# Row sums as two columns, inverted small and spread back over the partitions; attention logits moved ahead of X W2

## The reference, cut to what matters

```python
x = x + gnn(layernorm(x), adj, ...)
x = x + ffn(layernorm(x), ...)          # Mamba: scan over 1024 channels x 16 states

def gnn(X, A, Wv, bv, aw, ab, Wk, bk):  # per batch, N = 128, d = 256
    Xw = X @ Wv + bv
    sj, si = Xw @ aw[:d, 0], Xw @ aw[d:, 0]
    e = leaky_relu(sj[:, None, :] + si[:, :, None] + ab[0], 0.2)
    alpha = A * exp(e)
    transition = alpha / (sum(alpha, axis=-1, keepdims=True) + 1e-12)
    H, Xk = 0, X
    for k in range(3):
        H = H + Xk @ Wk[k] + bk[k]
        Xk = transition @ Xk
    return relu(H)
```

## Time and profile before

| | |
|---|---|
| median of 3 runs | 3949.91 us (3949.03 to 3950.27) |
| profiled execution | 3946.52 us |
| its span, first to last instruction | 3944.4 us |
| granted TensorE clock, mean | 0.979 |
| VectorE busy | 3646.4 us |
| TensorE busy | 3506.4 us |
| GpSimd busy | 3451.7 us |
| ScalarE busy | 2830.4 us |

### The profile page before, as it was taken

How to read it: one execution, slowest core, us unless ns; L and a number is a source line. 1 busy time by engine, 2 the same in 40 slices (tenths; PEclk the granted TensorE clock), 3 DMA queues, 4 the chain that set the end, 5 groups by cost and what they waited for, 6 DMA issues and landing times. The chain is left out here.

```text
span 3944.4 us, 43314 instructions
## 1 busy us (share of the span) xinstructions
PE 3506.4 (89%) x10938; PEld 1931.7 (49%) x10938; DVE 3646.4 (92%) x3133; ACT 2830.4 (72%) x6002; POOL 3451.7 (88%) x1860
## 2 busy tenths in 40 slices
PE   6789899999899999899989899989899899899887
PEld 3545455545455444455444455444455444445443
DVE  0499999999999999999999999999999999999998
ACT  1477777777777877777877777877777777677775
POOL 0298889998889998889998889998889998889999
PEclk9899999999999999999999999999999999999999
DMA  2111101111101111101111101111100111100110
GB/s 106 50 53 56 55 9 50 53 55 55 55 8 50 52 55 55 55 14 45 53 55 55 55 16 42 52 55 55 55 21 37 53 55 55 55 26 28 49 49 8
DMA packets 50715, 183.77 MB, mean 47 GB/s; under 512 B 7340, under 2 KB 33204, under 8 KB 42068
## 3 DMA queue, kind: packets, MB, share of 16 engines
q1 hardware_dynamic: 48880, 174.17, 11.5%
q10 hardware_dynamic: 1636, 7.83, 0.5%
HBM read 164.15 MB, written 17.83 MB: 46 GB/s over the span
## 5 line engine op out<-in xcount | busy, mean ns | idle before, releaser
L407 POOL TENSOR_TENSOR st<-st,bc 128x1024 f32<-128x1024 f32 x1024 | 2399.2, 2360 | 310.6 <-DVE st L843 310.5
L843 DVE TENSOR_TENSOR_SCAN st<-dec,st 128x1024 f32<-128x1024 f32 x1024 | 2310.0, 2277 | 26.6 <-ACT dec L460 20.3
L668 PE MATMUL y_ps<-st,ident 128*128 128x512 f32 x4096 | 1984.9, 613 | 309.7 <-POOL st L407 308.3
L460 ACT ACTIVATE dec<-delta,decay 128x254 f32<-128x254 f32 x4096 | 1696.8, 467 | 623.6 <-DVE st L843 608.3
L668 PEld LDWEIGHTS y_ps<-st,ident 128*128 128x128 f32 x4096 | 745.1, 192 | 1178.9 <-issue 582.2
L831 DVE TENSOR_TENSOR st<-du,bc 128x1024 f32<-128x1024 f32 x736 | 884.6, 1202 | 4.0 <-ACT du L446 4.0
L398 POOL TENSOR_TENSOR st<-du_sb,bc 128x1024 f32<-128x1024 f32 x288 | 679.5, 2360 | 0.1
L869 DVE SCALAR_TENSOR_TENSOR u<-d_ps,chan,u 128x250 f32<-128x250 f32 (+2 forms) x768 | 308.7, 472 | 68.1 <-ACT u L500 68.0
L706 PE MATMUL d_ps<-xnT,wxz 128*128 128x256 f32 x1024 | 250.5, 388 | 55.5 <-DVE u L869 55.5
L706 PEld LDWEIGHTS d_ps<-xnT,wxz 128*128 128x128 f32 x1024 | 191.0, 191 | 157.0 <-DVE u L869 107.1
L718 PE MATMUL d_ps<-xnT,wxz 128*128 128x256 f32 x1024 | 247.3, 385 | 13.6 <-ACT zs L509 13.5
(11 more groups left out here) (98 smaller groups left out, 2452.4 us busy)
## 6 DMA issues: line engine op xcount, KB each, us to landing
bc<-bc_dram SPq DMA_DIRECT2D x64, 2048.0 KB, 9.5
xg<-x_dram SPq DMA_DIRECT2D x32, 256.0 KB, 11.4
x_dram<-xg SPq DMA_DIRECT2D x32, 256.0 KB, 2.0
last_x<-x_dram SPq DMA_DIRECT2D x32, 256.0 KB, 2.6
out_dram<-last_x SPq DMA_DIRECT2D x32, 256.0 KB, 2.2
bc<-w_inT_dram ACTq DMA_DIRECT2D x1, 4096.0 KB
adjt<-adjT_dram SPq DMA_DIRECT2D x32, 128.0 KB, 11.1
bc<-w_out_dram ACTq DMA_DIRECT2D x1, 2048.0 KB
```

The costliest lines, as they stand in the source:

```text
L407: nc.gpsimd.tensor_tensor(st[:, sl, :, :, :], st[:, sl, :, :, :], bc[:, p, 1, SU * q:SU * q + SU, None, :].to_broadcast([P, SU, 2, T]), AL ...
L460: a = nc.scalar.activation(dec[:, v % 2, s, j, :].rearrange("p (b t) -> p b t", b=PAIR)[:, :, 1:], delta[:, p, 2 * i + j, :].rearrange("p ...
L668: mm = nc.tensor.matmul(y_all, ident[:, :], st[:, sl, s, :, :].rearrange("p j t -> p (j t)"), start=False, stop=(q == Q - 1 and s == SU - ...
L843: nc.vector.tensor_tensor_scan(h, dec[:, v % 2, :, :, :].rearrange("p s j t -> p (s j t)"), h, 0.0, ALU.mult, ALU.add).then_inc(S["scanned ...
```

## The change

The logits, exponentials and the product with the adjacency come first (phases 9, 11, 12). The row sums become two products with `att` of one batch as the stationary operand and one column of ones, so that they stand as two columns, one row per partition (phase 14). VectorE adds epsilon and inverts 128 x 2 elements (phase 15). X W2 follows (phase 16). ScalarE makes for each batch a diagonal matrix of the reciprocals in `xn` by scaling the identity (phase 17), then copies `x2k` (phase 18). TensorE multiplies ones with the diagonals, which spreads the reciprocals over all partitions (phase 19), and VectorE multiplies them into `att` (phase 20). The later phases move by one: 22 and 23, 25, 26 and 27, 29. ScalarE's second normalisation also waits for the spreading product, since the diagonals stand in `xn`.

```diff
         x1k = sb("x1k", [P, PAIR, DIM])
         x2k = sb("x2k", [P, PAIR, DIM])
         ones = sb("ones", [P, P])
+        rowsum = sb("rowsum", [P, PAIR])
+        rinv = sb("rinv", [P, PAIR])
         last_x = sb("last_x", [P, PAIR, DIM])
         bstat = sb("bstat", [P, PAIR, 6])
         mv = sb("mv", [P, PAIR, 2])
...
                     second = v == 33
                     wait(act, "rstd_made", 2 * g + 1 + second)
                     wait(act, "transposed", 2 * g + second)
+                    if second:
+                        wait(act, "rinv_mm", g + 1)
                     for b in range(PAIR):
                         a = nc.scalar.activation(xn[:, b, :], xg[:, p, b, :], ACT.Identity, bias=shift[:, b:b + 1],
                                                  scale=rstd[:, b:b + 1])
...
                     wait(act, "transposed", 2 * g + 1)
                     nc.scalar.activation(xT[:, :, :].rearrange("p c t -> p (c t)"), g0[:, :], ACT.Copy)\
                         .then_inc(S["xT_made"], 1)
-                if v == 11:
+                if v == 18:
                     wait(act, "x2k_mm", g + 1)
                     nc.scalar.activation(x2k[:, :, :].rearrange("p b d -> p (b d)"), g0[:, :], ACT.Copy)\
                         .then_inc(S["x2k_made"], 1)
-                if v == 14:
+                if v == 17:
+                    wait(act, "rinv_made", g + 1)
+                    for b in range(PAIR):
+                        a = nc.scalar.activation(xn[:, b, 0:P], ident[:, :], ACT.Copy, scale=rinv[:, b:b + 1])
+                    a.then_inc(S["rinv_diag"], 1)
+                if v == 11:
                     wait(act, "e_mm", g + 1)
                     nc.scalar.activation(att[:, :, :].rearrange("p b i -> p (b i)"), g0[:, 0:T], ACT.Exp, bias=c0[:, 0:1])
                     nc.scalar.activation(g0[:, T:2 * T], g0[:, 0:T], ACT.Exp, bias=c0[:, 1:2], scale=0.2)\
                         .then_inc(S["e_exp"], 1)
-                if v == 24:
+                if v == 25:
                     wait(act, "x1k_mm", g + 1)
                     nc.scalar.activation(x1k[:, :, :].rearrange("p b d -> p (b d)"), g0[:, :], ACT.Copy)\
                         .then_inc(S["x1k_made"], 1)
...
                             mm = nc.tensor.transpose(g0[:, c * T + b * L:c * T + (b + 1) * L],
                                                      xn[:, b, c * P:(c + 1) * P], ident[:, :])
                     mm.then_inc(S["transposed"], 1)
-                if v == 9:
-                    wait(pe, "xT_made", g + 1)
+                if v == 16:
+                    wait(pe, "rinv_made", g + 1)
                     for b in range(PAIR):
                         mm = hop(b, 2, True, True)
                     mm.then_inc(S["x2k_mm"], 1)
-                if v == 12:
-                    wait(pe, "x2k_made", g + 1)
+                if v == 9:
+                    wait(pe, "xT_made", g + 1)
                     for b in range(PAIR):
                         for c in range(KC):
                             cols = xT[:, c, b * L:(b + 1) * L]
...
                             mm = nc.tensor.matmul(g0[:, b * L:(b + 1) * L], cols, wj_rep[:, c, :],
                                                   start=False, stop=(c == KC - 1))
                     mm.then_inc(S["e_mm"], 1)
-                if v == 17:
+                if v == 14:
                     wait(pe, "alpha_made", g + 1)
-                    nc.tensor.matmul(g0[:, 0:T], ones[:, :], att[:, :, :].rearrange("p b i -> p (b i)"),
-                                     start=True, stop=True).then_inc(S["rowsum_mm"], 1)
-                if v in (21, 22):
-                    b = v - 21
+                    for b in range(PAIR):
+                        mm = nc.tensor.matmul(g0[:, b:b + 1], att[:, b, :], ones[:, 0:1], start=True, stop=True)
+                    mm.then_inc(S["rowsum_mm"], 1)
+                if v == 19:
+                    wait(pe, "x2k_made", g + 1)
+                    wait(pe, "rinv_diag", g + 1)
+                    for b in range(PAIR):
+                        mm = nc.tensor.matmul(g0[:, b * L:(b + 1) * L], ones[:, :], xn[:, b, 0:P], start=True, stop=True)
+                    mm.then_inc(S["rinv_mm"], 1)
+                if v in (22, 23):
+                    b = v - 22
                     wait(pe, "att_made", g + 1)
                     hop(b, 1, True, False)
                     mm = nc.tensor.matmul(g0[:, b * DIM:(b + 1) * DIM], att[:, b, :], x2k[:, b, :],
                                           start=False, stop=True, skip_group_check=True)
                     if b == 1:
                         mm.then_inc(S["x1k_mm"], 1)
-                if v in (25, 26):
-                    b = v - 25
+                if v in (26, 27):
+                    b = v - 26
                     wait(pe, "x1k_made", g + 1)
                     if b == 0:
                         nc.tensor.matmul(g0[:, :], ones3, bk_row, start=True, stop=False, skip_group_check=True)
...
                     for b in range(PAIR):
                         a = nc.vector.bn_aggr(mv[:, b, :], bstat[:, b, :])
                     a.then_inc(S["aggr"], 1)
-                if (v, late) == (15, 1):
+                if (v, late) == (12, 1):
                     wait(dve, "e_exp", g + 1)
                     nc.vector.tensor_tensor(g0[:, 0:T], g0[:, T:2 * T], att[:, :, :].rearrange("p b i -> p (b i)"),
...
                     nc.vector.tensor_tensor(att[:, :, :].rearrange("p b i -> p (b i)"), g0[:, 0:T],
                                             adjt[:, p, :, :].rearrange("p b i -> p (b i)"), ALU.mult)\
                         .then_inc(S["alpha_made"], 1)
-                if (v, late) == (19, 1):
+                if (v, late) == (15, 1):
                     wait(dve, "rowsum_mm", g + 1)
-                    nc.vector.tensor_scalar(g0[:, 0:T], g0[:, 0:T], EPS_ROW, None, ALU.add)\
+                    nc.vector.tensor_scalar(rowsum[:, :], g0[:, 0:PAIR], EPS_ROW, None, ALU.add)\
                         .then_inc(S["rowsum_eps"], 1)
                     wait(dve, "rowsum_eps", g + 1)
-                    nc.vector.reciprocal(g0[:, T:2 * T], g0[:, 0:T]).then_inc(S["rinv_made"], 1)
-                    wait(dve, "rinv_made", g + 1)
-                    nc.vector.tensor_tensor(att[:, :, :].rearrange("p b i -> p (b i)"), g0[:, T:2 * T],
+                    nc.vector.reciprocal(rinv[:, :], rowsum[:, :]).then_inc(S["rinv_made"], 1)
+                if (v, late) == (20, 1):
+                    wait(dve, "rinv_mm", g + 1)
+                    nc.vector.tensor_tensor(att[:, :, :].rearrange("p b i -> p (b i)"), g0[:, 0:T],
                                             att[:, :, :].rearrange("p b i -> p (b i)"), ALU.mult)\
                         .then_inc(S["att_made"], 1)
-                if (v, late) == (28, 0):
+                if (v, late) == (29, 0):
                     wait(dve, "h_mm", g + 1)
                     x1 = xg[:, p, :, :].rearrange("p b d -> p (b d)")
                     nc.vector.scalar_tensor_tensor(x1, g0[:, :], 0.0, x1, ALU.max, ALU.add).then_inc(S["x1_made"], 1)
```

More of the change, by code:

```diff
@@ L175, in build @@
         dec_zeroed diag_made x_loaded adj_loaded stats aggr veps_made rstd_pow rstd_made normed transposed xT_made xnT_made
-        x2k_mm x2k_made e_mm e_exp alpha_max alpha_made rowsum_mm rowsum_eps rinv_made att_made x1k_mm x1k_made
+        x2k_mm x2k_made e_mm e_exp alpha_max alpha_made rowsum_mm rowsum_eps rinv_made rinv_diag rinv_mm att_made x1k_mm x1k_made
         h_mm x1_made x1_stored x1_reloaded
```

## The result

The kernel after takes 3984.92 us (median of 4 runs, 3983.60 to 3985.47) against 3949.47 us before: ratio 1.009, interval 1.0073 to 1.0108. It is slower by 35 us; the forecast was 3943.6 us. Its profiled span is 3982.6 us, 38.2 us more than before.

The account below looks back on a forecast made before the run. The bound was taken as a loop: GpSimd's 80.4 us, 4.9 us over TensorE and ScalarE, VectorE for the rest. Steps 3 to 7 (-6.0) and the fill (-0.3) turn 3949.9 into 3943.6 us; range 3933 to 3959.

Parts of the forecast that it names:

- The new waits: Column sums at TensorE's step 24, spreading product at 29: VectorE waits 1 to 1.6 us at step 30, costing nothing.
- the hinge: Body's end: GpSimd's product of unit 30, TensorE's sum and u, ScalarE's bias, VectorE's taps of step 1; forecast not later.
- the residual: L942 on VectorE moves behind scan 6 and fills idling before the taps of step 7: -0.45 us a body.
- the fill: Bodies -3 to -1, where the graph chain is late: +1.5, -1.0 and -0.8, sum -0.3 us, bounds -3 and +3.
- GpSimd's 80.4 us: GpSimd's unbroken stretch from the product of unit 8 to that of unit 30, part of the loop setting a body's 118 us.
- VectorE's saving: 1868 ns a group, 59.8 us in all, at steps 25 to 30, before existing idling at step 1: worth zero.
- Rival (a): VectorE is the bound and its saving arrives: 3884 us, or in part 3890 to 3935; chance 0.11, whole or in part.
- The steps 3 to 7: Critical stretch: the copy +0.25, the residual -0.45, sum -0.20 us a body, -6.0 us over 30 bodies.
- the copy: ScalarE's `x1k` copy moves from step 2 to step 3, behind the gate activation: taps of step 5 come 0.25 us later.
- Rival (b): The copy at step 3 delays the taps 0.30 us a body, L942's move gives nothing: +9.0 us, 3959 us; chance 0.12.
- Rival (c): New handovers stall VectorE until GpSimd starves: 3974 us at 1 us beyond a wait of some 3 us; chance 0.07.
- The first term's sum: Body -3 in the fill: decay exponential ends at 78.83; copy 0.6, product 0.7, multiplication 0.4 give 80.6; net +1.5 us.

Follow-up runs that it names:

- e3_before_late: Kernel before with only the last phases one step later (22 and 23, 25, 26 and 27, 29), row sums and logits untouched: 3984.21 us.
- e1_late_back: Kernel after with its last phases back at their old places (21 and 22, 24, 25 and 26, residual at 28): 3953.47 us.
- e4_x1_at_29: As e1_late_back, but the residual stays at phase 29, between scans 6 and 7: 3932.34 us.
- e2_filler: Kernel after plus an unread product of X with W1 for one batch, about 1 us on TensorE, at step 31: 3941.90 us.
- e5: e4_x1_at_29 with the gate product moved from ahead of scan 2 to ahead of scan 3, and X W0 with the second hop at 26 and 27: 3935.07 us.
- e10: e4_x1_at_29 with the gate product alone moved from ahead of scan 2 to ahead of scan 3: 3970.98 us.
- e7: e4_x1_at_29 plus two unread VectorE reciprocals at phase 19, about 3.5 us a group: 3943.51 us.
- e9_before_x1_29: Kernel before with one edit, the residual at phase 29 instead of 28: 3933.94 us.
- e6_pad_1: e4_x1_at_29 plus one unread VectorE reciprocal of 128 x 256 at phase 19: 3932.18 us.

## Why the prediction was wrong

**The step that failed** is in "The new waits": "TensorE's step 31 becomes free and its work goes behind u of step 0, so the hinge is not later." I counted free time on TensorE as harmless. It was, as a queue; it was not as a clock. The pause ahead of the sum grew from 1.35 to 2.62 us, the sum and u behind it took 1.70 us more (the sum alone from 1.98 to up to 3.68), and these two are the place in the body where TensorE is on the critical path. The missing term is +1.70 us x 28 = +47.6 us. e3_before_late shows that moving the last phases makes the loss without the inversion, e1_late_back that moving them back removes it, e4_x1_at_29 that the residual has no part in it, and e2_filler that the work's use does not matter, only that it is there.

**The clock** was in the prediction, for the fill, where it was allowed 1.9 us. I did not carry it to the earlier trace rows, where a pause stood in front of a critical product. The trace of the kernel before had the warning: behind a pause of 2.64 us in the middle of the body the sum is slow in 17 of the bodies 1 to 28 (last section).

**What bounds the kernel** was right. GpSimd's 80.4 us, the hinge and VectorE's steps 1 to 8 add up to a body in every kernel here. In some bodies of e5 and e10 a late sum of TensorE reaches into GpSimd's stretch, and in ten bodies of e7 VectorE's own work is late at the hinge.

**VectorE's saving is worth zero**: right, and shown three ways. e1_late_back has it and equals before, within 0.0015. e9_before_x1_29 lacks it and equals e4_x1_at_29. e6_pad_1 puts 1.7 us a group back at no cost. Rival (a) falls with that: the engine at 92%, the highest share of all, can be relieved of 56.5 us for nothing.

**The steps 3 to 7**: the copy +0.24 (forecast +0.25), the residual -0.55 (forecast -0.45), together -0.32 in place of -0.20 a body. Without the clock's term the kernel after is e2_filler, 3941.9 us against the forecast 3943.6. That is closer than the terms deserve: the steady part gained 9.6 us in place of 6.0, and in its profile the first taps of body 0 start 4.7 us later than before, where the forecast had 0.3 earlier. Rival (b) falls: the residual's move gave its gain.

**The new waits**: VectorE waits 0.77 us at step 30 of a steady body (forecast 1 to 1.6), and nobody waits for it. GpSimd's stretch from unit 8 to unit 1 has no gap. Rival (c) falls.

**The fill**: the first taps of body 0 start 1.26 us later than before (183.55 against 182.29), forecast 0.3 earlier, within its bounds. (The first term's sum, 78.83 plus 0.6, 0.7 and 0.4, is 80.5 and not 80.6.) Over the profiles of all kernels this point lies between 182.3 and 189.4 us, also where the fill's edits are the same, so one profile says little about a term of this size.

**The range** left out the truth because no rival had TensorE's clock in it at the hinge. The chance of 0.13 for slower stood on two mechanisms that are both refuted; that slower came out gives them no credit.

## What to carry to other kernels

When an edit moves work off an engine that waits, look at what the engine does next and whether that is on the critical path; for TensorE the pause in front of it is part of its price (in these runs 1.92 us and more could put the lower clock level behind it), and a product that nobody reads can be cheaper than an empty step. Look for it over several bodies: one row can show full speed where the next body is slow, and a mean clock hides it. Before costing a saving, find the loop that sets a body's length: an engine at 92% that idles for 0.9 us in front of the hinge gives nothing back. Where an engine of the critical stretch idles for half a microsecond, look for an instruction of its own that may stand there: that was worth some 17 us for one number in the source, where the large edit gave nothing.

## What the runs showed that I had not expected

At the hinge the clock held in all steady bodies over pauses of 1.35 and 1.77 us. Over those of 2.20, 2.5 and 2.62 us it fell in 27 or 28 bodies of each run. Ahead of e10's late sums 1.92 us were enough in nineteen bodies and not in ten. The length alone does not decide. In the kernel before, ahead of the sum of unit 6, TensorE pauses for 2.64 us in every body. In the bodies 1 to 28 the sum is slow behind it in 17, up to 3.60 us, and at full speed in 11. Bodies 5 and 7:

```profile
799.33 3.60 PE L668 MATMUL y_ps<-st,ident 128*128 128x512 f32 x4 [2.64 <-POOL st L407]
```

```profile
1035.51 1.98 PE L668 MATMUL y_ps<-st,ident 128*128 128x512 f32 x4 [2.64 <-POOL st L407]
```

A body takes 118.1 us with the one and with the other, so it costs nothing there. In the kernel after a pause of 2.04 us at the corresponding place is followed by a slow sum in bodies 1 to 13 and by one at full speed in bodies 14 to 28. Body 7:

```profile
1043.77 2.61 PE L678 MATMUL y_ps<-st,ident 128*128 128x512 f32 x4 [2.04 <-POOL st L409]
```

And at the hinge of the kernel after the pause is 2.6 us in bodies 0 and 29 as well, and the sum takes 1.99 and 1.98. So at these places pauses up to 1.77 us never brought the fall, and those from 1.92 us on could; something else decides whether it comes and where, since its place drifts against the sum from body to body. What else enters was not tried.
